# First attention: the first tokens loaded and split ahead, and half of them handed on before the last unit ends

## The reference

```python
x = x + _L0_attn_ref(_layernorm(x), w_attn, b_attn, w_proj, b_proj)
#   q, k, v = split(x @ w_attn + b_attn); 16 heads of 8
#   scores = q @ k.T * 8 ** -0.5 - log(distance + 1), causal; softmax; @ v; @ w_proj + b_proj
x = x + _L0_ffn_ref(_layernorm(x), w_gate, w_up, w_down)
#   (silu(x @ w_gate.T) * (x @ w_up.T)) @ w_down.T, integer weights scaled by 1/127
```

## Time and profile before

| | |
|---|---|
| median of 3 runs | 1104.17 us (1096.57, 1104.17, 1106.09) |
| profiled execution | 1102.42 us, span of the trace 1100.3 us |
| TensorE's granted clock, mean | 0.887 of full speed |
| PE busy | 896.0 us (81%) |
| DVE busy | 665.8 us (61%) |
| POOL busy | 512.2 us (47%) |
| ACT busy | 427.8 us (39%) |

### The profile page before, as it was taken

How to read it: one execution, slowest core, us unless ns; L and a number is a source line. 1 busy time by engine, 2 the same in 40 slices (tenths; PEclk the granted TensorE clock), 3 DMA queues, 4 the chain that set the end, 5 groups by cost and what they waited for, 6 DMA issues and landing times. The chain is left out here.

```text
span 1100.3 us, 17965 instructions
## 1 busy us (share of the span) xinstructions
PE 896.0 (81%) x6334; PEld 606.8 (55%) x6334; DVE 665.8 (61%) x1876; ACT 427.8 (39%) x1024; POOL 512.2 (47%) x463
## 2 busy tenths in 40 slices
PE   4668999999999867267899699994998987389992
PEld 2122333333333356155566588994895756389982
DVE  6767778686872075879687656778003666533334
ACT  2323665565666441113111276774334211032220
POOL 5425888888898831053222344555200001156661
PEclk9657999899999988758799799997999998599997
DMA  4800110110000000001000000302000001266764
GB/s 146 257 1 1 31 31 2 30 30 19 13 2 24 1 22 8 0 15 40 1 2 1 10 21 10 134 9 77 1 1 1 1 10 30 89 188 216 217 196 145
DMA packets 38893, 55.95 MB, mean 51 GB/s; under 512 B 6954, under 2 KB 26290, under 8 KB 38678
## 3 DMA queue, kind: packets, MB, share of 16 engines
q1 hardware_dynamic: 36310, 49.70, 14.9%
q0 software_dynamic: 2496, 5.12, 1.6%
HBM read 43.66 MB, written 10.94 MB: 50 GB/s over the span
## 5 line engine op out<-in xcount | busy, mean ns | idle before, releaser
L423 POOL TENSOR_TENSOR arena<-arena 128x1024 f32<-128x1024 f32 (+3 forms) x105 | 201.0, 1946 | 42.4 <-ACT arena L598 42.3
L665 DVE CUSTOM_DVE_ANT_0 ps<-ps,arena 128x512 f32<-128x512 f32 (+3 forms) x256 | 148.7, 640 | 45.3 <-PE ps L480 44.4
L598 ACT ACTIVATE arena<-ps 128x512 f32<-128x512 f32 (+3 forms) x320 | 137.3, 491 | 89.4 <-PE ps L511 58.1
L480 PE MATMUL ps<-arena 48*128 48x512 bf16 (+3 forms) x384 | 103.9, 371 | 24.9 <-DVE arena L665 15.9
L117 POOL TENSOR_SCALAR vareps<-meanvar 128x4 f32<-128x4 f32 x32 | 7.9, 246 | 213.2 <-DVE meanvar L98 213.2
L503 PE MATMUL ps<-arena 51*128 51x512 bf16 (+3 forms) x384 | 76.0, 349 | 6.0 <-DMA arena<-arena 5.2
L2075 PE MATMUL ps<-arena 128*128 128x128 f32 x624 | 79.9, 284 | 0.0
L480 PEld LDWEIGHTS ps<-arena 48*128 48x128 bf16 x384 | 28.3, 95 | 91.3 <-DVE arena L665 55.1
L2075 PEld LDWEIGHTS ps<-arena 128*128 128x128 f32 x624 | 76.4, 200 | 0.0
L152 PE MATMUL ps<-ident,xn 128*128 128x128 f32 x128 | 26.0, 352 | 59.4 <-DVE x L921 19.9
L532 PE MATMUL ps<-arena 128*9 128x512 f32 (+3 forms) x640 | 67.7, 495 | 3.9 <-POOL arena L423 3.9
(11 more groups left out here) (341 smaller groups left out, 2081.0 us busy)
## 6 DMA issues: line engine op xcount, KB each, us to landing
arena<-in_L_ffn_w SPq DMA_DIRECT2D x39, 512.0 KB, 3.7
arena<-scratch SPq DMA_DIRECT2D x32, 192.0 KB, 4.0
arena<-in_L_ffn_w SPq DMA_DIRECT2D x16, 256.0 KB, 3.4
scratch<-arena SPq DMA_DIRECT2D x12, 256.0 KB, 4.4
arena<-expert_rows SPq DMA_DIRECT2D x8, 256.0 KB, 4.9
scratch<-arena SPq DMA_DIRECT2D x4, 384.0 KB, 5.0
scratch<-arena SPq DMA_DIRECT2D x12, 128.0 KB, 4.3
x<-in_x SPq DMA_DIRECT2D x4, 256.0 KB, 3.9
```

Source lines behind the costliest of these rows:

```text
L423: nc.gpsimd.tensor_tensor(e, e, weight[:, at:at + k].unsqueeze(1).broadcast_to([P, 2, k]), ALU.mult).then_inc(weighed, 1)
L480: nc.tensor.matmul(m.ps[:, (2 * k + e) % MAX_BANKS, 0:wd], qs[rows, u % BUFS, pair, i * P:(i + 1) * P], ks[rows, u % BUFS, pair, first:fir ...
L598: nc.scalar.activation(probs(g)[:, 2 * p + e, 0:wd], m.ps[:, BANK[h, e], 0:wd], ACT.Exp, scale=SCALE).then_inc(exps, 1)
L665: nc.vector.tensor_tensor_reduce(out=scores, in0=scores, in1=before[:, 0:wd], scale=-1.0, scalar=negrest[:, h, i:i + 1] if i < TPC else 3e ...
```

## The change

**The start.** SP loads chunk 0, `ident`, chunk 1, then `w`, `bqk`, `bv` (their own semaphore, `first_in`), then the rest. PE's first transpose waits for these alone. DVE normalises chunks 0 and 1 as soon as their statistics are there, and takes the statistics of chunks 2 and 3 within the splitting of batch 0. `turn_to` makes PE transpose two chunks together. Batch 1's parts get memory of their own (`parts_of[1]`, in two buffers of the ring of probabilities), so ACT no longer waits for `parts_out[0]`. SP issues only unit 0's reads ahead of batch 1's writes, and those of units 1 and 2 behind them. POOL begins the log steps after batch 0 is split, and `add_bias` comes behind them.

**Mid-loop.** The feed-forward's weights are loaded ahead of the loop, and ACT widens them in three instructions in unit 3.

**The last unit.** Batch 0's outputs are complete once unit 3's last numerators are divided. In unit 7, from half 164 on, chunks 0 and 1 are transposed, copied, projected, added, counted and normalised; POOL computes their two roots at half 172. `shares` allows 2600 for that and gives POOL none of the last 8 halves. The loop's POOL halves are the same up to half 171; after it 172, 173, 183, 184, 185, 187, 188, 190 and 191 pass from POOL to PE, and 174 from PE to POOL. `oT` has a buffer for each chunk.

**The feed-forward.** Chunks 0 and 1 are turned and copied between the end of attention and its first product; chunks 2 and 3 are normalised behind its first and third product on DVE.

```diff
     def wait_xnT(self, pe, c):
         nc, m = self.nc, self.m
-        if self.turned == 0:
+        if self.turned == 0 and self.k == 0:
+            pe.wait_ge(m.set_up, 2)
+            pe.wait_ge(m.ident_in, 16)
+        elif self.turned == 0 and not self.before.ahead:
             pe.wait_ge(*self.before.ready[NC - 1])
-            if self.k == 0:
-                pe.wait_ge(m.set_up, 2)
-                pe.wait_ge(m.consts_in, 16 * (2 + len(BIASES)))
-        while self.turned < min(c + 2, NC):
+        self.turn(pe, self.turn_to[c])
...
+    parts_of = [parts, ring[:, 2:4, :, :].rearrange("p a h n -> p (a h n)")[:, 0:6 * CH].bitcast(BF16).rearrange("p (a j n) -> p a j n", a=3, j=2)]
...
+    oT = [a[:, n * CH:(n + 1) * CH] for a in (logw, masked) for n in range(S // CH)]
+    EARLY = NC // B
+    Y_BANK = (0, 1, 4, 5)
...
+    norm.turn_to = [(c // QC + 1) * QC for c in range(NC)]
...
+    LAST_BY_POOL = UNITS * HALVES - 8
+    ROOTS_AT = window(UNITS - 1)[1] + 14
+    PREPARE_AT, PREPARED = 3 * HALVES + 2, 3
...
+            if h == ROOTS_AT:
+                pool += 2600
-            if pool + (1500 if diagonal(n) else 0) <= gone:
+            if pool + (1500 if diagonal(n) else 0) <= gone and h < LAST_BY_POOL:
...
+        for c in range(EARLY):
+            at = window(UNITS - 1)[1] + 6 + c
+            due[at].append(("turn_o", UNITS - 1, c))
+            due[at + 1].append(("take_o", UNITS - 1, c))
+            due[at + 3].append(("project", UNITS - 1, c))
+            due[at + 4].append(("add", UNITS - 1, c))
+            due[at + 12].append(("normalise", UNITS - 1, c))
+        for n in range(PREPARED):
+            due[PREPARE_AT + 2 * n].append(("prepare", 0, n))
...
             if c == QC - 1:
-                for u in range(BUFS):
-                    stack(sp, u)
+                stack(sp, 0)
+        for u in range(1, BUFS):
+            stack(sp, u)
+        following.load(sp)
...
+    def gpsimd(pool, following):
+        pool.wait_ge(low_set, 2 * QC)
         pool.wait_ge(w_in, w_all)
...
+                    if u * HALVES + 2 * n + p == ROOTS_AT:
+                        for c in range(EARLY):
+                            following.root(pool, c)
...
+            if (what, u, n) == ("times_v", UNITS - 1, NG - 1):
+                following.turn(pe, EARLY)
+        for c in range(EARLY, NC):
+            turn_outputs(0, c)
+        for c in range(EARLY, NC):
+            project(0, c)
...
-            if n == 2 * QC:
-                act.wait_ge(parts_out[0], OUT)
-            norm.copy_xnT(act, n // 2 + 1)
+            norm.copy_xnT(act, norm.turn_to[n // 2] - 1)
...
+        following.copy(act, 0)
+        for c in range(EARLY, NC):
+            take_outputs(0, c)
+        for c in range(1, EARLY):
+            following.copy(act, c)
...
+        norm.statistics(dve, 0)
+        norm.statistics(dve, 1)
+        norm.normalise(dve, 0)
+        norm.normalise(dve, 1)
         left_of_high(0)
...
+            if n in (1, 3):
+                norm.statistics(dve, n // 2 + QC)
...
             if n + 1 == 2 * QC:
+                norm.normalise(dve, QC)
+                norm.normalise(dve, QC + 1)
                 left_of_high(n + 1)
```

More of the change, by code:

```diff
@@ L45, in __init__ @@
         self.banks, self.bias_late = (6, 7), False
+        self.inside, self.turn_to = False, [min(c + 2, NC) for c in range(NC)]
         self.split, self.splits_before = None, m.splits
-        self.counted_stats = self.counted_xn = self.turned = self.copied = 0
+        self.counted_stats = self.counted_roots = self.counted_xn = self.turned = self.copied = 0
     def value(self, c):
@@ L114, in gpsimd @@
         for c in range(NC):
[L115 to L120 removed]
+            if c >= self.before.ahead:
+                while self.counted_roots < NC:
+                    self.root(pool, self.counted_roots)
             if self.split:
@@ L438, in gpsimd @@
         nc.gpsimd.tensor_tensor(log_low, logw[:, :], log_high.bitcast(F32), ALU.subtract).then_inc(log_steps, 1)
+        for c in range(NC):
+            norm.add_bias(pool, m.bias_of["L0_attn_b_proj"], c)
         for u in range(UNITS):
@@ L593, in exp @@
             wd = width(n)
+            if g == 3 and p == 0:
+                act.wait_ge(parts_out[B - 1], OUT)
             if g >= RING:
@@ L616, in scalar, with vector @@
                 do[what](u, n)
-        for c in range(NC):
-            act.wait_ge(o_turned, c + 1)
-            if c:
-                act.wait_ge(y_mm, c)
-            nc.scalar.activation(oT, m.ps[:, c, :], ACT.Copy).then_inc(oT_set, 1)
-    def vector(dve, after):
+            if what == "prepare":
+                act.wait_ge(parts_out[B - 1], OUT)
+                following.prepare[n](act)
+        following.copy(act, 0)
[3 more added lines that the diff above has]
+            following.copy(act, c)
+    def vector(dve, following):
         def left_of_high(n):
@@ L725, in l0_ffn @@
     m.rounded.fresh()
+    norm.banks = (2, 1, 7, 6)
     x_high, x_low = norm.split_xnT()
@@ L761, in down @@
                 pe.wait_ge(x_done, norm.done(c - 2))
+            else:
+                pe.wait_ge(*norm.before.ready[c + 2])
             for f in range(FT):
@@ L2445, in _ @@
                         sp.wait_ge(*built[k - 2][1].ready[c])
-                if part.sync:
+                if part.ahead:
+                    part.sync(sp, following[id(norm)])
+                elif part.sync:
                     part.sync(sp)
@@ L2458, in _ @@
                     part.before_norm["tensor"](pe)
-                if part.tensor:
+                if part.ahead:
+                    part.tensor(pe, following[id(norm)])
+                elif part.tensor:
                     part.tensor(pe)
@@ L2466, in _ @@
                     part.before_norm["vector"](dve)
-                norm.vector(dve)
-                part.vector(dve, after(norm))
+                if not (norm.before.ahead or norm.inside):
+                    norm.vector(dve)
+                part.vector(dve, following[id(norm)] if part.ahead else after(norm))
         @block.scalar
@@ L2474, in _ @@
                     part.before_norm["scalar"](act)
-                part.scalar(act)
+                if part.ahead:
+                    part.scalar(act, following[id(norm)])
+                else:
+                    part.scalar(act)
         @block.gpsimd
@@ L2484, in _ @@
                 norm.gpsimd(pool, m.bias_of.get(part.bias))
-                if part.gpsimd:
+                if part.ahead:
+                    part.gpsimd(pool, following[id(norm)])
+                elif part.gpsimd:
                     part.gpsimd(pool)
```

156 lines of the change are left out of this document (91 added, 65 removed).

## The result

| | before | changed |
|---|---|---|
| median of 20 runs | 1102.16 us | 1096.08 us |
| lowest to highest | 1093.23 to 1114.87 | 1087.60 to 1100.73 |
| profiled execution | 1102.42 us | 1096.22 us |
| granted clock in that execution | 0.887 | 0.874 |

The ratio is 0.9951, with an interval of 0.9929 to 0.9973: 5.4 us faster, where 13.5 were forecast. The time lies inside the range of 1080 to 1099, but the gain is 0.4 of the sum's, and the prediction had put 0.64 on a gain of over 1%. Four more comparisons, on four chips, gave 0.9939, 0.9942, 0.9935 and 0.9915. The plain mean of the five is 0.9936, which is 7.0 us; weighted by their intervals it is 6.5 us.

What follows compares the result with a forecast made beforehand. With TensorE busy 18.3 of 20 us in a loop left as it is, gains lay at the two ends: 1102.42 - 4.1 - 9.4 = 1088.9, forecast 1090 us, own range 1084 to 1096, overall range 1080 to 1099.

Steps and rivals of the forecast that it cites:

- The start: Ahead of the loop: first projection at 10.2 instead of 15.18, batch 1 at 29.0, maxima and loop 4.1 us early.
- the row at 33.16: Start of the kernel before: read as PE taking up batch 1 after 5.5 us idle; now forecast at 29.0.
- The lock: Skill's port rule at the start: log step holds DVE 2.79 us, normalising costs 5.0, start wins 3.2 instead of 4.1.
- the clash: Chunks 2 and 3 normalised beside POOL's first log step: 4.1 us, against 2.2 without a clash.
- The last unit: End of the loop: PE gets 6.0 us more work, some waits for POOL go; division ends 2.3 us later.
- the trade of halves: Last unit: nine halves leave POOL, one returns; PE's matmuls grow by 0.92 and 2.5 us, against waits of 3.9.
- The hand-over: From last numerators but one to end of division 6.2 us or so; DVE's first feed-forward product at 391.2, 9.4 early.
- taking nothing for its normalisings: Feed-forward: DVE normalises two chunks (2.2 us) between products, in earlier gaps; counted as nothing, 2 us at worst.
- the sum itself: Whole kernel: profiled 1102.42 less 4.1 at the start and 9.4 at the tail gives 1088.9; forecast placed at 1090.
- a loop that differs by more than one or two dips of 5 us: Sign of being wrong: the granted clock in the loop differs by more than that.
- slower: Rival: low clock lasts some 54 us longer from the loop's start, turning 13.5 us won into 11 lost; 1115, chance 0.05.
- It does nothing that shows: Rival: gains at both ends are lost or the clock takes them back; 1098 to 1104, chance 0.06.

Runs made afterwards that it cites:

- pool_keeps: Changed kernel with the bound on the last 8 halves taken out, so POOL weighs some of them as before; 0.9946 of the kernel before.
- filler: Changed kernel with extra TensorE matmuls, whose result nobody reads, in and behind unit 0's maxima; 0.9938 of the kernel before.
- delay10: Changed kernel with 17 unread VectorE reductions ahead of the feed-forward's first product, leaving TensorE idle there; 1.0015 of the kernel before.
- no_clash: Changed kernel with POOL's first log step waiting until chunk 3 is normalised; 0.9902 of the kernel before.
- the mended kernel: Changed kernel with POOL's log step waiting for chunk 3's normalising and the last 8 halves open to POOL; 0.9889, then 0.9868 of the kernel before.

## Why the prediction was right and wrong

**The start** was right as a whole. First projection 10.49 (forecast 10.2), memset 36.86 (36.6). Between them two errors cancelled, and the agreement is in part luck. Normalising two chunks took 3.40 us (4.1), and batch 1 began at 26.72, 2.3 us before the forecast 29.0, since batch 0's split ended at 22.4 and not 24.1. But from there to the memset took 10.1 us, where the prediction counted 7.5. It had misread the row at 33.16. TensorE had made chunk 2's products at 24.85, and they waited for ScalarE, which waited for batch 0's parts to land; 33.16 is chunk 3's. In the kernel before:

```profile
24.85 1.88 PE L453 MATMUL ps<-xnT,arena 128*128 128x512 f32 x4
...
32.51 0.60 ACT L165 ACTIVATE xnT<-ps 128x512 f32<-128x512 f32 x1 [7.03 <-DMA scratch<-arena]
33.01 1.26 ACT L567 ACTIVATE arena<-ps,arena 128x512 bf16<-128x512 f32 x2
```

In the changed kernel ScalarE takes them up when TensorE has made them:

```profile
28.68 0.69 ACT L630 ACTIVATE arena<-ps,arena 128x512 bf16<-128x512 f32 x1 [1.11 <-PE ps L508]
```

So the like-for-like step is ScalarE's first split of batch 1, 33.01 against 28.68, 4.3 us early, and the memset comes 3.8 us early. In all five traces of the changed kernel A is 37.3 to 38.8 us, and 39.8 to 41.1 before, so the start is worth 2.4 on average, where 4.1 was forecast.

**The lock.** The Trainium skill (SBUF — State Buffer, "SBUF: two separate sides") says that an instruction of GpSimd and one of VectorE that needs the shared ports exclude each other: whichever starts first holds them for its whole length and the other is fully blocked. The trace shows a clash, but not this rule. Three of VectorE's eight instructions took 0.9 to 1.1 us instead of 0.34, and the other five their usual time. Four that had begun after the log step (22.87 to 24.38) ended while it ran, the last of them 0.9 us before its end at 25.61. A full block would have held them until then. The profile's spans on GpSimd are rough, but VectorE's own times show no hold longer than 1.1 us. The price was 1.26 us and not 2.79. The forecast of 4.1 us for the two chunks had taken 1.9 for the clash, from its rows.

**The last unit** was forecast 2.3 us longer and is (45.6 to 47.9), 3.3 by the mean of the five traces (47.9 and four of 48.8 to 48.9, against 45.3 to 45.6); those four had 3.4 us of low clock there, the first none. The part that was wrong is the trade of halves: it was taken to remove 3.9 us of waits for POOL at 3.4 us of TensorE's time (0.9 and 2.5), and `pool_keeps` shows that only 1.1 us of such waits is left when POOL keeps five of the eight.

**The hand-over**: from the end of the last division it took 6.5 us (6.2). The first product came at 390.46, 3.4 later than the forecast 387.1: 2.7 of it is the loop's, 0.3 the hand-over's, 0.3 the start's. The feed-forward's own stretch took 21.0 us (21.3 before), so taking nothing for its normalisings was right.

**The step that failed is the sum itself**: "1102.42 - 4.1 - 9.4 = 1088.9" lets every untouched stage keep its time. In the first pair of traces they took 6.9 us back: B, F and G were 2.7, 0.6 and 4.7 us longer, with 10, 4 and 12 us more at the low clock. The prediction had named a loop that differs by more than one or two dips of 5 us as a sign of being wrong, and 10 us is that. The size is best taken from all runs. By the means of the five traces after and three before, the touched stretches save 2.4 - 3.3 + 11.1 + 0.4 = 10.6 us instead of 13.5: 1.7 of the shortfall is the start's and 1.0 the last unit's. The five comparisons show 6.5 to 7.0, so some 4 us are lost elsewhere. The clock accounts for part of that at most. The mean granted clock of the runs is lower in the changed kernel in three of the four later comparisons, 0.8811 against 0.8839, 0.8822 against 0.8838 and 0.8796 against 0.8805, and higher in the fourth, 0.8845 against 0.8827, which is also the one with the largest gain (0.9915). Over all runs of these kernels time falls by about 790 us per 1.0 of mean clock, which makes 2.2, 1.3 and 0.7 us lost and 1.4 won, 0.7 lost on average. A further part lies in where the low clock falls. The hand-over had 8 us of it in the kernel before, while TensorE mostly waited, and none now; by the traces' record the start has 5 us more of it now. What is left, 2 us or so, is inside the intervals.

**The rivals.** The "slower" one named low clock in the loop, with a price of 2.3 us in 5, or 0.46 us per us; it wanted 54 us more of it to turn the sign, and got 10 in the first trace and about 12 on the mean (35.5 in B before, 48 to 51 in the changed kernel). Its place, the loop's start, was right in the first trace alone; in the other four the added low clock lies later. The price was near: over the 19 traces (all but `filler`'s) B is 247.5 us plus 0.38 for each us of low clock, F 87.4 plus 0.37, G 146.6 plus 0.36, and no trace is off its line by more than about 1 us. It should have stood as a small deduction in every case instead of as a rival of 0.05. "It does nothing that shows" came half true.

**What stays open.** It is shown that B, F and G last longer by 0.36 to 0.38 us for each us of low clock. It is not shown that the change brings more of it. For a debt that idle time pays speak the falling row of F and G and the time of `delay10`; the 20 of 29.5 us are too uncertain to tell, the mean clock of `delay10` speaks against it, and `pool_keeps`, `no_clash` and the mended kernel have F and G of 262.6 to 267.9 us without idle time. Chance speaks for the rest: the profiled executions of the kernel before ran from 0.3 us above to 7 below the medians of their runs, and those of the changed kernel 0 to 7 above theirs. By the means of the traces the changed kernel would be 2 us slower as a whole, where its runs are 6.5 to 7 faster. So differences between traces in B, F and G overstate the effect. What sets where the low clock falls was not found.

## What to carry to other kernels

Where TensorE is the bound and its clock changes level, read the granted clock of the untouched stretches, price it (here 0.36 to 0.38 us per us at the low level), and don't take for granted that they keep their time when a gap of TensorE is removed: here 6.5 to 7 of 10.6 us came through, for a reason that is open. Before a step of a sum is taken from a row, make sure which piece of work the row is; here one chunk's projection was read as another's. Before work is handed from one engine to another to remove a wait, count what else the change puts into that wait; here the output work had probably filled it, and the hand-over of halves cost 1.7 us in its stretch. Sums of steps from one trace came within 1 to 2 us of the stretch that they described, but one execution's loop varied by 12 us, so judge what a change is worth by the ratio of many runs.

## What the chip showed that I had not expected

- Two executions of one program differed by 12.2 us in the loop (259.2 and 271.4 us, clocks 0.94 and 0.88), but by only 1.2 us in the whole span (1088.0 and 1089.2). 5.2 us of the difference came back in F and G, 106.7 and 161.2 us in the one and 104.1 and 158.6 in the other, and 5.3 in the stretch behind G.
- The low clock does not only stand behind idle time. In the first trace of the changed kernel it went on from 70 to 121 us, with TensorE busy 45.67 of 49.80 us, and the rest of the loop then ran at 1.00; in four later traces of the same program it ended at 91 to 92 us and came back in dips of 3 to 10 us.
- Low clock cost nothing where another engine was the bound. Stretch C of the kernel before, where GpSimd is the busiest engine (29.00 of 29.00 us), took 45.3 us with 10.2 us of low clock in it and 45.6 with 1.6. So the mean clock of a run tells its time only where the low clock lies in the same places: `filler`'s runs had 0.8846 against 0.8811 for the changed kernel beside them, in the same time.
